# A turn of the heads in 48 steps of one projection product each, with new places for all operations of all engines

## The reference

```python
q = silu(causal_dwconv(x @ Wq, qcw, qcb)); k = silu(causal_dwconv(x @ Wk, ...)); v = silu(causal_dwconv(x @ Wv, ...))
alpha = sigmoid(x @ Wa + ba); beta = sigmoid(x @ Wb + bb)
def step(S, inps):                       # over the 2048 tokens of a sequence
    qt, kt, vt, at, bt = inps
    Sk = einsum('bhvk,bhk->bhv', S, kt)
    S = at * S - bt * ((Sk - vt)[..., None] * kt)
    return S, einsum('bhvk,bhk->bhv', S, qt)
o = layernorm(o) * ln_w + ln_b
o = o * sigmoid(x @ Wg)
return o @ Wo
```

## Time and profile before

| | us |
|---|---|
| median of three runs | 3584.06 (3581.86 to 3584.07) |
| span of the profiled execution | 3583.2 |
| PE busy | 3503.4 (98%) |
| PE's weight loads busy | 2910.6 (81%) |
| DVE busy | 2418.1 (67%) |
| ACT busy | 2318.2 (65%) |
| POOL busy | 1958.7 (55%) |

### The profile page before, as it was taken

How to read it: one execution, slowest core, us unless ns; L and a number is a source line. 1 busy time by engine, 2 the same in 40 slices (tenths; PEclk the granted TensorE clock), 3 DMA queues, 4 the chain that set the end, 5 groups by cost and what they waited for, 6 DMA issues and landing times. The chain is left out here.

```text
span 3583.2 us, 105506 instructions
## 1 busy us (share of the span) xinstructions
PE 3503.4 (98%) x32276; PEld 2910.6 (81%) x32276; DVE 2418.1 (67%) x5757; ACT 2318.2 (65%) x6479; POOL 1958.7 (55%) x4932
## 2 busy tenths in 40 slices
PE   8999979999999999999999999999999999999999
PEld 6777768888888888888888888888888888877887
DVE  5655557777777777777777777777777777753222
ACT  4444357777777777777777777777777777752111
POOL 2444346666666666666666666666666666653000
PEclk9999999999999999999999999999999999999999
DMA  8644433323333333333533333333333333454453
GB/s 290 232 172 162 164 90 76 79 76 76 82 88 81 79 76 77 82 81 76 149 99 77 84 79 77 77 76 78 84 77 78 76 76 77 108 157 128 141 147 111
DMA packets 427681, 375.88 MB, mean 105 GB/s; under 512 B 191984, under 2 KB 323056, under 8 KB 421248
## 3 DMA queue, kind: packets, MB, share of 16 engines
q1 hardware_dynamic: 424000, 362.46, 37.1%
q0 software_dynamic: 2080, 6.82, 0.5%
q10 hardware_dynamic: 1056, 0.02, 0.0%
HBM read 292.62 MB, written 76.58 MB: 103 GB/s over the span
## 5 line engine op out<-in xcount | busy, mean ns | idle before, releaser
L1312 DVE SCALAR_TENSOR_TENSOR conv<-bank,tap,conv 128x512 f32<-128x512 f32 x1152 | 861.7, 748 | 153.9 <-ACT conv L1448 123.4
L1138 POOL TENSOR_TENSOR prods<-Lb,Tc 128x60 f32<-128x60 f32 (+14 forms) x1920 | 478.7, 249 | 606.3 <-DMA Lb<-base_d 462.0
L1518 PE MATMUL bank<-hx_hi,w_hi 128*128 128x512 f32 x1536 | 665.4, 433 | 0.0
L1518 PE MATMUL bank<-hx_hi,w_lo 128*128 128x512 f32 x1536 | 645.1, 420 | 20.2 <-DVE Tnb L1274 16.7
L1518 PE MATMUL bank<-hx_lo,w_hi 128*128 128x512 f32 x1536 | 638.3, 416 | 0.0
L1145 POOL TENSOR_TENSOR Tc<-Tc,prods 128x56 f32<-128x56 f32 (+13 forms) x1792 | 458.9, 256 | 141.4 <-POOL prods L1138 1.9
L1429 ACT ACTIVATE Wc<-bank 128x128 f32<-128x128 f32 x512 | 140.9, 275 | 373.6 <-PE bank L1620 332.0
L1518 PEld LDWEIGHTS bank<-hx_hi,w_lo 128*128 128x128 f32 x1536 | 292.9, 191 | 58.7 <-DVE Tnb L1274 24.6
L1266 DVE SCALAR_TENSOR_TENSOR S<-S,gamma,bank 128x128 f32<-128x128 f32 x480 | 167.0, 348 | 235.5 <-PE bank L1631 221.1
L1518 PEld LDWEIGHTS bank<-hx_hi,w_hi 128*128 128x128 f32 x1536 | 292.4, 190 | 39.2 <-DVE conv L1312 2.5
L1518 PEld LDWEIGHTS bank<-hx_lo,w_hi 128*128 128x128 f32 x1536 | 292.8, 191 | 29.4
(11 more groups left out here) (199 smaller groups left out, 8913.7 us busy)
## 6 DMA issues: line engine op xcount, KB each, us to landing
Lb<-base_d SPq DMA_DIRECT2D x128, 512.0 KB, 4.7
gamma<-gamma_d SPq DMA_DIRECT2D x128, 258.0 KB, 3.6
alpha<-alpha_d SPq DMA_DIRECT2D x128, 256.0 KB, 3.3
oT_d<-oG SPq DMA_DIRECT2D x128, 256.0 KB, 4.5
gu_raw<-in_gate_up SPq DMA_DIRECT2D x16, 1408.0 KB, 6.3
o_raw<-oT_d SPq DMA_DIRECT2D x13, 1024.0 KB, 6.8
w_raw<-oT_d SPq DMA_DIRECT2D x12, 1024.0 KB, 7.2
dn_raw<-in_down SPq DMA_DIRECT2D x44, 256.0 KB, 6.9
```

What stands on the lines that cost most here:

```text
L1138: pool.tensor_tensor(prods[:, :, i + 1:], Lb[:, i, :, i + 1:], Tc[:, :, i:i + 1].to_broadcast([P, G, SB - 1 - i]), ALU.mult)\
L1312: dve.scalar_tensor_tensor(out=conv[i][:, to], in0=PJ[PJ_OF[g][i]][:], scalar=tap[:, i, j + 1:j + 2], in1=conv[i][:, to], op0=ALU.mult, op ...
L1518: last = pe.matmul(dst, a[:, i, k], b[:, k], start=(j == 0), stop=(j == 3 * KC - 1))
```

## The change

Only the table of constants changes. `STEPS` goes from 38 to 48, so each step has one projection product where before ten steps had two, and all operations get new steps:

```diff
-STEPS = 38
+STEPS = 48
-CHAIN = {0: 0, 7: 1, 8: 2, 11: 3, 15: 4, 18: 5, 19: 6, 22: 7, 23: 8, 26: 9, 28: 10, 36: 11}
+CHAIN = {0: 0, 4: 1, 12: 2, 15: 3, 17: 4, 19: 5, 24: 6, 27: 7, 31: 8, 35: 9, 40: 10, 47: 11}
-A_AT, KT_AT, VT_AT, ON_TURN_AT, L_AT = 4, 1, 9, 22, 18
-VISIT_AT = {20: 0, 1: 1}
+A_AT, KT_AT, VT_AT, ON_TURN_AT, L_AT = 9, 0, 16, 27, 22
+VISIT_AT = {26: 0, 0: 1}
...
```

More of the change, by code:

```diff
@@ L56 @@
             [(1, 1), (1, 2), (1, 3), (0, 0)], [(1, 1), (1, 2), (1, 3), (0, 1)]]
-A_AT, KT_AT, VT_AT, ON_TURN_AT, L_AT = 4, 1, 9, 22, 18
-VISIT_AT = {20: 0, 1: 1}
[L59 to L70, removed]
+A_AT, KT_AT, VT_AT, ON_TURN_AT, L_AT = 9, 0, 16, 27, 22
+VISIT_AT = {26: 0, 0: 1}
+SOLVE_AT = {45: (0, 1), 3: (1, 2), 5: (2, 4), 6: (4, 5), 8: (5, 7), 11: (7, 8), 12: (8, 10), 16: (10, 15)}
+T16P_AT, POW_AT, QG_AT, OG_AT, DIAG_AT, LC_AT = 17, 19, 21, 23, 21, 20
+AT_AT, K_AT, T16_AT, TN64_AT, DECAY_AT, LT_AT = 10, 1, 19, 6, 18, 20
+BN_AT, AGGR_AT, ON_AT = 0, 9, 24
+YB_AT, TT_AT = 34, 3
+CONV_AT = {14: (0, 0), 15: (0, 1), 16: (0, 2), 25: (1, 0), 27: (1, 1), 31: (1, 2), 37: (2, 0), 44: (2, 1), 46: (2, 2)}
+VSILU_AT, GATE_AT, DIAGB_AT, VROWS_AT, KSILU_AT, QSILU_AT, OT_AT = 0, 34, 13, 18, 19, 36, 32
+PLACE_AT = {33: (0, 1), 5: (2, 3)}
+TN_PLACE_AT = 6
+MT32_AT, TT64_AT, MT64_AT, TT128_AT = 47, 4, 39, 4
+O_AT = {10: 0, 20: 1, 34: 2, 0: 3}
+TAP_AT = {6: 0, 22: 1, 35: 2}
 TILES, TILE0 = 6, 4
-TILE_CUT_AT = {20: (0, 1), 26: (1, 1), 33: (2, 1), 4: (3, 0)}
-TILE_AT = 2
-CUT_AT = {(3, 13): 0, (3, 21): 1, (3, 28): 2, (0, 19): 3}
+TILE_CUT_AT = {25: (0, 1), 33: (1, 1), 42: (2, 1), 5: (3, 0)}
+TILE_AT = 3
+CUT_AT = {(3, 21): 0, (3, 26): 1, (3, 35): 2, (0, 20): 3}
 ROUND_E, ROUND_T, RING = 4, 11, 3
```

## The result

The kernel with the new table takes 3619.4 us (median; 3614.9 to 3620.9) where the kernel before takes 3584.1. The ratio is 1.0098, with a 95% interval of 1.0084 to 1.0113. The forecast was 3570 us with a range to 3592: the sign was wrong, and the time lies outside the range. The profiled execution spans 3618.0 us against 3583.2.

What follows compares the result with a forecast made beforehand. The prediction took a closed loop of waits through six engines, the matrix inversion's 21.41 us a turn, as the bound. From 3584.1 us it took 8 for PE being late for `LT` and 6 in the tile turns: 3570, range 3545 to 3592.

Runs made afterwards that it cites:

- e1_mt32: The changed kernel with ACT's four MT32 copies at step 33 instead of 47, ahead of the fourth chunk's Wc: 3654.8 us, ratio 1.0192.
- e2_cuts: The changed kernel with the first weight cut at step 14 instead of 21, the third at 44 instead of 35, MT32 at 41 instead of 47: 3710.4 us.
- a2_cut: The changed kernel with the fourth turn's first weight cut at step 14 on ACT and 18 on GpSimd, instead of 21: 3701.9 us, ratio 1.0319.
- a6_tap: The changed kernel with PE's second visit at step 2 instead of 0, chain product 1 at 9 instead of 4, ACT's tap at 9 instead of 6: 3605.5 us.
- a8_mend: a6_tap with DVE's BN statistics at step 4 instead of 0, k_rows at 4 instead of 1, the second weight cut at 28 instead of 26: ratio 0.9993.

## What to carry over

When a change gives an operation a new place, list for it and for its reader the new distance, over the wrap of the loop too, and look at the turn in which the producing engine has the most queued ahead: a bound in one turn of four costs its full length there, and slack in the other three pays nothing back. In a table of steps a number orders the operations of one engine and says nothing of time: what stands ahead of an operation, and what that waits for, decides. Leaving a piece of the suspected bound out is the quickest way to learn how far away the next one is.

## What the runs showed of the hardware

In e1_mt32 PE stood idle twice in short order, 0.64 us behind the wait for Wc and then 0.41 us. Some 1.8 us after it went on, its products started 0.43 us apart instead of 0.23, for some 3.4 us, as from 2.4 to 1.2 GHz:

```profile
775.91 0.49 PE L1637 MATMUL bank<-Wc,AT 128*128 128x128 f32 x2 [0.64 <-ACT Wc L1429]
776.81 0.50 PE L1518 MATMUL bank<-x_hi,w_hi 128*128 128x512 f32 x1 [0.41 <-issue]
...
779.13 0.63 PE L1518 MATMUL bank<-x_hi,w_lo 128*128 128x512 f32 x1
779.55 0.63 PE L1518 MATMUL bank<-x_hi,w_hi 128*128 128x512 f32 x1
```

The record of the granted clock shows the same at the same time, 0.50 from 778.61 to 782.02 (the column behind POOL's):

```profile
778.61:782.02 3.41, 3.41 (x11) 2.85 (x10) 2.20 (x10) 1.98 (x8) 2.63 (x11) 0.50 0.28 44
```

This came in 13 of the 30 late turns of e1_mt32. Counted from L1685 to L1685, those 13 take 24.55 us on average and the other 17 take 23.14, so one such stretch costs 1.4 us, and the 13 cost 18 of the 31 us that the turns of this run lost against the changed kernel. Turns of both kinds have a gap of 0.6 us and then one of 0.4 or 1.0, so the gaps alone do not settle in which turn the clock falls; what does is not shown. In e2_cuts it fell in 22 of 30 late turns (26.30 us with, 24.63 without) and in a2_cut in 17 (26.15 and 24.51). In the turns of the changed kernel, whose single wait of 1.0 us stands in the same place, the granted clock never fell, nor did it in a6_tap or a8_mend. So a wait on PE can cost more than its length.
